# Scores from transposed projections: query and key layout taken from the token-wise product, squares on GpSimd

## What is computed

```
q = split_heads(tokens @ Wq, HEADS)
kv = split_heads(tokens @ Wkv, HEADS)
k, v = (kv[..., :DK], kv[..., DK:])
q, k, v = (l2norm(q), l2norm(k), l2norm(v))
sim = jnp.einsum('bhid,bhjd->bhij', q, k)
attn = jnp.square(jax.nn.relu(sim))
out = jnp.einsum('bhij,bhjd->bhid', attn, v)
out = tanh_norm(out)
return out @ Wout
```

## Time and profile before

| | |
|---|---|
| three runs | 568.56, 570.13, 570.86 us (median 570.13) |
| the profiled execution | 570.36 us, of which 568.4 us are the span from the first to the last instruction |
| attention | about 22 to 229 us of the span, after a head of 22 us |
| busy in the whole span | PE 93%, DVE 75%, ACT 66%, POOL 58% |
| busy from 97 to 122 us (25.0 us) | PE 23.9, DVE 20.5, ACT 18.5, POOL 14.9 us |
| one batch in the steady stretch | 26.88 us (score(13) starts at 98.76, score(17) at 125.64) |

### The profile page before, as it was taken

One profiled execution on the slowest core, in us unless ns is written; L12 is line 12 of the kernel. 1 busy time (PEld: TensorE's weight loads), 2 busy tenths in 40 slices (PEclk: granted clock), 3 DMA queues, 4 the chain that ended last, 5 costly groups with the idle time before them and its releaser, 6 DMA issues. The chain is left out here.

```text
span 568.4 us, 10116 instructions
## 1 busy us (share of the span) xinstructions
PE 529.2 (93%) x3280; PEld 399.7 (70%) x3280; DVE 428.1 (75%) x1004; ACT 376.8 (66%) x675; POOL 327.7 (58%) x277
## 2 busy tenths in 40 slices
PE   5798799999999998899999999999999999999996
PEld 4565467576666665586887877887887887888884
DVE  5966978888879687559679778778778778777664
ACT  5697868777778875264465864864864864755653
POOL 2643929384856564186565756656656655565553
PEclk9899989999999999799999999999999999999999
DMA  8200000000000002910192761851851851861920
GB/s 227 81 18 15 21 15 17 15 15 15 16 16 22 11 21 76 211 29 1 36 217 52 174 132 30 197 104 28 201 101 29 200 118 31 189 127 50 215 56 18
DMA packets 36083, 44.73 MB, mean 79 GB/s; under 512 B 5440, under 2 KB 18880, under 8 KB 36032
## 3 DMA queue, kind: packets, MB, share of 16 engines
q1 hardware_dynamic: 31616, 42.53, 32.9%
q10 hardware_dynamic: 4416, 1.57, 1.2%
HBM read 40.94 MB, written 3.15 MB: 78 GB/s over the span
## 5 line engine op out<-in xcount | busy, mean ns | idle before, releaser
L493 POOL TENSOR_TENSOR hl<-hb,hh 128x512 fp32r<-128x512 f32 x128 | 165.4, 1293 | 137.7 <-ACT hh L703 134.7
L696 ACT ACTIVATE sil<-PS 128x512 f32<-128x512 f32 (+1 forms) x136 | 80.9, 595 | 90.1 <-PE PS L1196 89.3
L1075 DVE TENSOR_TENSOR PS<-sil,PS 128x512 f32<-128x512 f32 x128 | 88.4, 690 | 62.4 <-PE PS L1196 41.4
L1196 PE MATMUL PS<-fxh,wfh 128*128 128x512 f32 x264 | 104.9, 397 | 1.7 <-issue 1.7
L1196 PE MATMUL PS<-fxl,wfh 128*128 128x512 f32 x264 | 104.6, 396 | 0.0
L1196 PE MATMUL PS<-fxh,wfl 128*128 128x512 f32 x264 | 104.3, 395 | 0.0
L703 ACT ACTIVATE hh<-hb 128x512 fp32r<-128x512 f32 x128 | 80.2, 627 | 28.2 <-DVE hb L1080 27.8
L1080 DVE TENSOR_TENSOR hb<-PS,wbc 128x512 f32<-128x512 f32 x128 | 88.5, 691 | 9.2 <-DMA wbc<-w_dram 2.5
L854 DVE SCALAR_TENSOR_TENSOR aT<-PS,rl 128x1024 f32<-128x1024 f32 x64 | 75.2, 1217 | 9.1 <-ACT rl L559 9.1
L559 ACT ACTIVATE rl<-PS 128x1024 f32<-128x1024 f32 x64 | 62.3, 1031 | 22.3 <-PE PS L1196 21.7
L418 POOL TENSOR_TENSOR sr<-n2o,half 128x32 f32<-128x32 f32 x7 | 38.2, 5463 | 51.1 <-DVE n2o L861 51.1
(11 more groups left out here) (168 smaller groups left out, 905.8 us busy)
## 6 DMA issues: line engine op xcount, KB each, us to landing
wbc<-w_dram SPq DMA_DIRECT2D x48, 512.0 KB, 11.7
wbc<-w_dram SPq DMA_DIRECT2D x32, 128.0 KB, 2.9
wbc<-w_dram SPq DMA_DIRECT2D x16, 256.0 KB, 4.3
wfs<-wf_dram SPq DMA_DIRECT2D x32, 98.0 KB, 1.9
band_dram<-zero SPq DMA_DIRECT2D x16, 80.0 KB, 1.7
band<-band_dram ACTq DMA_DIRECT2D x4, 320.0 KB, 3.0
out_dram<-X SPq DMA_DIRECT2D x4, 256.0 KB, 2.3
X<-x_dram SPq DMA_DIRECT2D x1, 896.0 KB, 7.7
```

Of the source, the lines that this page charges most:

```text
L493: g.tensor_tensor(hl[:, n % RING, :], hb[:, n % RING, :], hh[:, n % RING, :].bitcast(F32), ALU.subtract).then_inc(F("hl"), 1)
L696: s.activation(sil[0:rows, n % 2, :], PS[0:rows, G0 + n % 2, :], ACT.Silu).then_inc(F("silu"), 1)
L1075: v_.tensor_tensor(PS[:, bank, :], sil[:, n % 2, :], PS[:, bank, :], ALU.mult).then_inc(F("t"), 1)
L1196: return nc.tensor.matmul(o, w, m, start=start, stop=stop)
```

## The change

The second projection goes. ACT copies the token-wise product to a new SBUF tile `qkt` (`keep_pairs`): queries into 32-wide slots whose other halves POOL has set to zero once, keys side by side. PE transposes 128 × 128 pieces of `qkt` into PSUM: four transposes for each `group(n, j)` in place of six products. The squares are no longer made by ACT from PSUM: for batches 1 to 7 POOL makes them from `qkt` (`square_pairs`, four instructions of 256 columns per batch); for batch 0 ACT makes them as before, after its copies (`first_square_pairs`). `pair_norms` on DVE moves from behind `squares(4b + 1)` to behind `squares(4b + 2)`. 768 columns of weights are neither loaded nor split any more. The keys stand in another order, so `vc` is read through another view.

```diff
@@ POOL
+            g.memset(qkt[:, :, 0:NG * QG], 0.0).then_inc(cs("qkz"), 1)
             g.memset(Fpad[:, :, :], 0.0).then_inc(cs("fpad"), 1)
...
+            def square_pairs(n, t):
+                pool.wait_ge(A("qkc"), 2 * n + t + 1)
+                pool.wait_ge(A("n2q"), 2 * (n - 1) + t + 1)
+                g.tensor_tensor(by_head(sqqk[:, t, 0:QK]), q_heads(t), q_heads(t), ALU.mult).then_inc(A("sqq"), 1)
+                pool.wait_ge(*freed("qk", n, t))
+                g.tensor_tensor(sqqk[:, t, QK:2 * QK], k_heads(t), k_heads(t), ALU.mult).then_inc(A("sqq"), 1)
...
                 if b + 2 < B:
                     inverse_deviation(b + 2)
+                if b + 1 < B:
+                    square_pairs(b + 1, 0)
+                    square_pairs(b + 1, 1)
                 if b:
                     output_norms(b - 1)
@@ ACT
-            def square_pairs(n, t):
+            def keep_pairs(n, t):
                 act.wait_ge(*full("qk", n, t))
-                after(act, A("n2q"), 2 * (n - 1) + t + 1)
-                s.activation(sqqk[:, t, :], PS[:, bank_of("qk", n, t), :], ACT.Square).then_inc(free_of("qk", n, t), 1)
+                if n:
+                    act.wait_ge(*full("g", n - 1, NQ - 1))
+                    after(act, A("sqq"), 4 * (n - 2) + 2 * t + 2)
+                bank = bank_of("qk", n, t)
+                s.activation(q_heads(t), by_head(PS[:, bank, 0:QK]), ACT.Copy).then_inc(A("qkc"), 1)
+                signal = free_of("qk", n, t) if n else A("qkk0")
+                s.activation(k_heads(t), PS[:, bank, QK:2 * QK], ACT.Copy).then_inc(signal, 1)
+
+            def first_square_pairs(t):
+                s.activation(sqqk[:, t, :], PS[:, bank_of("qk", 0, t), :], ACT.Square).then_inc(free_of("qk", 0, t), 1)
...
-            first_weights_high(3)
...
-            square_pairs(0, 0)
-            square_pairs(0, 1)
+            act.wait_ge(cs("qkz"), 1)
+            for t in range(2):
+                keep_pairs(0, t)
+            for t in range(2):
+                first_square_pairs(t)
             square_values(0, 1)
@@ DVE
             def pair_norms(n, t):
-                dve.wait_ge(*freed("qk", n, t))
+                if n:
+                    dve.wait_ge(A("sqq"), 4 * (n - 1) + 2 * t + 2)
+                else:
+                    dve.wait_ge(*freed("qk", 0, t))
...
                 squares(NG * b + 1)
-                if more:
-                    pair_norms(n, 0)
-                    pair_norms(n, 1)
...
                 squares(NG * b + 2)
                 if more:
+                    pair_norms(n, 0)
+                    pair_norms(n, 1)
                     value_norms(n, 0)
                     clear_norms(n, 0)
@@ PE, group(n, j)
                 for part in range(2):
-                    cols = slice((2 * j + part) * P, (2 * j + part + 1) * P)
-                    last = split3(PS[:, bank, part * L:(part + 1) * L], wah[:, cols], wal[:, cols],
-                                  xTh[:, :], xTl[:, :])
+                    cols = k_cols(part) if j == 1 else q_cols(j + part)
+                    for t in range(2):
+                        last = nc.tensor.transpose(PS[:, bank, part * L + t * P:part * L + (t + 1) * P], qkt[:, t, cols],
+                                                   ident[:, :])
                 last.then_inc(done, 1)
```

More of the change, by code:

```diff
@@ L202, in hybrid_layer @@
         Z = Sems(ctx, nc, "full0 full5 full6 full7 free0 free5 free6 free7")
-        ld = Sems(ctx, nc, "in_x0 in_x in_wv0 in_wv1 in_wq in_wp in_wo in_wf0 in_wf1 in_sd in_gw in_wb in_bb zeroed")
-        cs = Sems(ctx, nc, "id0 id half rid ind0 ind rm rf sel fpad zero sel1 sdz wah wal wfh wfl sdh sdl")
-        A = Sems(ctx, nc, "stats mv ve rstd xn xTh vraw sqv n2v n2q nm nm_v rr vi vc0 vc vp S relu a av Oc sqO "
+        ld = Sems(ctx, nc, "in_x0 in_x in_wv0 in_wv1 in_wp in_wo in_wf0 in_wf1 in_sd in_gw in_wb in_bb zeroed")
+        cs = Sems(ctx, nc, "id0 id half rid ind0 ind rm rf sel fpad zero sel1 sdz wah wal wfh wfl sdh sdl qkz")
+        A = Sems(ctx, nc, "stats mv ve rstd xn xTh vraw sqv n2v n2q nm nm_v rr vi vc0 vc vp qkc qkk0 sqq S relu a av Oc sqO "
                           "sr sr_half n th nmx rec f1 ff fhi f")
@@ L299, in hybrid_layer, with q_cols, k_cols, q_heads @@
         fxh, fxl, wbc = (fxh0, fxh1), (fxl0, fxl1), (wbc0, wbc1)
+        def q_cols(g):
+            return slice(QG * g - DK * (g % 2), QG * g - DK * (g % 2) + P)
+        def k_cols(f):
+            return slice(NG * QG + f * P, NG * QG + (f + 1) * P)
+        def q_heads(t):
+            slots = qkt[:, t, 0:NG * QG].rearrange("p (g x) -> p g x", x=QG)[:, :, 0:P]
+            return slots.rearrange("p g (r y) -> p g r y", y=SLOT)[:, :, :, 0:DK]
+        def k_heads(t):
+            return qkt[:, t, NG * QG:QT]
+        def by_head(x):
+            return x.rearrange("p (g r d) -> p g r d", g=NG, r=HG)
+        def k_by_group(x):
+            return x.rearrange("p (f r a) -> p f a r", f=2, r=HG)
+        def heads_by_group(x):
+            return x.rearrange("p (f a r) -> p f a r", f=2, a=2)
         block = ctx.enter_context(nc.Block())
@@ L1231, in group @@
             def group(n, j):
+                for t in range(2):
+                    if j != 1:
+                        pe.wait_ge(A("qkc"), 2 * n + t + 1)
+                    elif n:
+                        pe.wait_ge(*freed("qk", n, t))
+                    else:
+                        pe.wait_ge(A("qkk0"), t + 1)
                 bank, done = turn("g", n, j)
                 for part in range(2):
[L1234 to L1236 removed]
+                    cols = k_cols(part) if j == 1 else q_cols(j + part)
+                    for t in range(2):
+                        last = nc.tensor.transpose(PS[:, bank, part * L + t * P:part * L + (t + 1) * P], qkt[:, t, cols],
+                                                   ident[:, :])
                 last.then_inc(done, 1)
@@ L1560, in layout @@
     wk, wv = wkv[:, :, :DK], wkv[:, :, DK:]
[L1561 to L1566, removed]
+    wa = np.concatenate([wq, wk.reshape(D, 2, 2, HG, DK).transpose(0, 1, 3, 2, 4).reshape(D, H * DK), wv.reshape(D, H * DV)], axis=1)
     eg = np.asarray(L0_ffn_expert_gate).transpose(2, 0, 1).reshape(D, E * I)
```

24 lines of the change are left out of this document (11 added, 13 removed).

## The result

The changed kernel takes **579.68 us** (median of four runs, 577.89 to 581.10); the kernel before, on the same chip, 570.41 (568.56 to 570.86). The ratio is 1.0167, with a 95% interval from 1.0129 to 1.0205: slower by 9.3 us. The forecast was 577.5 with a range from 572.0 to 583.5. The profiled execution took 580.3 us, of which 578.5 are span, 10.1 more than before.

What follows compares the result with a forecast made beforehand. The prediction took DVE's late add to X, not PE, as the bound. Head 1.85, batch 0 1.15, batch 1 0.55 and batches 2 to 6 3.6 sum to 7.15 us: 570.36 becomes 577.5, range 572.0 to 583.5.

Steps and rivals of the forecast that it cites:

- What bounds the kernel: Between 112 and 119 us of a batch a late DVE lengthens it; PE work saved ahead of 119 us gains nothing.
- the ring: DVE's first sqv sum, ACT's second squares, DVE's second sum: the moved sums' 1.18 us pass on, 1.15 at the add.
- Transposes at 0.48 us for a group: Four transposes replace 0.91 us of products; only group(n, 2) counts, saving 0.43, so batches 2 to 6 lose 0.72 each.
- Batch 0: PE waits for aT ahead of score(4), so all of the delay counts and no saving: +1.15 us.
- Batch 1: score(8) and relu(8) come 1.15 us late; 0.55 is left where PE waits for DVE: +0.55 us.
- The head: Before score(0): POOL's clearing delays DVE by 0.8 us, ACT's four copies add 1.03 at sqv; together +1.85.
- The signs named ahead: Profile after: second sqv sum 3.6 us behind aT, PE's wait near 2 us, steady batch 27.6, POOL idle near 3.
- POOL's squares free: Four instructions at 0.7 us end at 106.6, with 2.9 us in hand ahead of sr: cost nothing; slow-squares rival 0.06.
- What ends behind the add: output_factors' first small step (L866) starts later but ends at nearly the same time, with POOL's values: nothing more.
- the gap's case: Rival, chance 0.15: DVE's gap between its sqv sums takes up the moved sums; 573.4 us, 572.7 with a cheap clearing.
- The clock: Rival, chance 0.25: PE's 2.2 us idle in batches 2 to 6 drops the clock, 5 × 1.1 us more: 583.0.
- took the feed-forward for unchanged: The change leaves the feed-forward layers as they are; a changed time there would show the prediction wrong.

Runs made afterwards that it cites:

- e1: Kernel before with only pair_norms moved behind squares(4b + 2); products, ACT's squares and head as before: 577.08 us, ratio 1.0145.
- e9: Kernel before with a second buffer for the values' squares and nothing else: 569.71 us, ratio 1.0027.
- e4: Changed kernel with the transposes of groups 0 and 1 of each later batch issued three times over into the same bank: 575.95 us, ratio 1.0135.
- e10: Kernel before with a second buffer for the values' squares and ACT's second squares ahead of keep_output(4b + 1): 566.63 us, ratio 0.9969.
- e3: Changed kernel with POOL's clearing of qkt moved behind the first inverse deviation: 579.22 us, ratio 1.0196.
- e8: Changed kernel with each of POOL's four squares per batch made three times over: 580.23 us, ratio 1.0227.
- e7: Changed kernel with only POOL's clearing of qkt moved behind the third split of weights on DVE: 578.46 us, ratio 1.0186.
- e6: Changed kernel with pair_norms behind normalise, a second buffer for the values' squares, and POOL's clearing behind the third split of weights: 569.04 us, ratio 1.0004.
- e11: Changed kernel with pair_norms behind normalise, two value-square buffers, clearing behind the third weight split, ACT's second squares ahead of keep_output(4b + 1): 567.32 us, ratio 0.9980.
- e12: As e11, with DVE's weight_low(4b + 1) moved behind squares(4b + 3) and the add to X: 567.75 us, ratio 1.0010.

## Why the prediction was right, point by point

- **What bounds the kernel.** DVE between the first sum over `sqv` and the add to X, not PE. Held: with the sums back PE is idle for 0.94 us there, and 48 matmuls fewer did not make the kernel faster.
- **The delay goes through the ring whole.** Forecast 1.15 us at the add to X; in e1 PE's wait grew by 1.14, and the second buffer took out the gap. Held for the changed kernel. What the prediction read out of the kernel before, that DVE's own sum starts the squares it then waits for, is only half of it: there ACT's own list ends at the same time, since the second buffer alone gained nothing (e9).
- **Transposes at 0.48 us for a group.** Group(n, 2) to the score is 0.56 (128.22 to 128.78), and PE starts 0.42 us behind the start of the add to X where it started 0.33 behind. So the third group is worth 0.35 − 0.09 = 0.26 us a batch, not 0.43. This term was too large: batches 2, 4 and 6 are 0.87, 0.92 and 0.73 longer, and batches 3 and 5 without the clock 0.86 and 0.90. Together 4.28, forecast 3.6. The figure of the Trainium skill (TensorE: Matmul & The Clock Gate, Part 4: PE-mode transpose), 275 ns each, would have given 1.10 for a group; the trace does not bear it out.
- **Batch 0.** Forecast 1.15, measured 1.11. **Batch 1.** Forecast 0.55. Two runs without a fall of the clock in these batches price it: score(4) to score(8) is 25.37 us in e4 and 24.24 before; score(8) to score(10) 13.04 in e4 and 13.61 in e10 (that e10 stands there for the kernel before at full clock is an estimate: the two differ only in the gap on DVE). 1.13 − 0.57 = 0.56. Held.
- **The head.** Forecast 1.85 = 0.8 + 1.03. The first transposes come 0.85 later, and from the last product to score(0) it is 4.12 − 3.09 = 1.03 more. The other 0.11 of 1.99 go with the time at which PE's products change speed. The sizes held, but the way to the 0.8 was another: DVE was not seen to wait for `ind0`; its four `sel` steps took 1.67 us under the clearing (0.67 in e3, where only two clearings of 0.31 and 0.15 us ran beside them), and the next step follows without idle time. The clearing held them up as well as `ind`, which ends at 3.03. The trace does not part the two. Who moves only the order on POOL meets the same thing one step later, as e3 did.
- **The signs named ahead.** The second sum over `sqv` starts 3.5 us behind the end of `aT` (forecast 3.6; 118.84 + 1.22 = 120.06, and 123.57), PE waits 2.06 us ahead of group(n, 2) (near 2), the steady batch at full clock is 27.75 us (27.6), read from e4 and e8, since in the changed kernel's own profile batches 3 and 5 hold a fall.
- **POOL's squares free.** They start 0.57 us apart, forecast 0.7, and 3.45 us are left ahead of `sr`, forecast 2.9. Held, with room for eight more. They do lengthen DVE's normalising step beside them to 1.08 us (112.85) from 0.59, but DVE waits 3.10 us for PE behind it.
- **What ends behind the add.** The step that took 1.40 us in the earlier trace rows (L866, now L912) takes 0.28 and ends at 128.27. POOL's scaling of the values ends at 126.33 + 1.91 = 128.24, 0.03 us ahead of it as before (120.46 and 120.49). Nothing came from there, as forecast.

The terms without the clock give 1.88 + 1.11 + 0.56 + 4.28 = 7.8 us, forecast 7.15. One slip in the prediction changes nothing here: it takes 572.0 as the low end of the gap's case, which by its own sum is 572.7.

- **The clock, held as a rival at 0.25, was partly true.** It fell behind the add's wait in two of five batches: behind 2.06 us at 98.93 and 2.48 us at 156.39, not behind 2.06 at 128.22 and 185.74 or 0.99 at 213.68. In batch 1 it was at the lower level for longer than before. Against e4's 13.04 and e10's 13.61 the stretch from score(8) to score(10) lost 2.67 us in the changed kernel (15.71) and 1.13 in the kernel before (14.74). With 0.11 in the head, 0.17 between score(4) and score(8) (25.54 against e4's 25.37) and the two falls of 1.54 and 1.55 it is 0.11 + 0.17 + 1.54 + 1.54 + 1.55 = 4.9 us more than before, and then 2.6 less at the entry of the feed-forward: 2.3 net, which with 7.8 is the 10.1 of the spans. What the sum had wrong is that it put the clock at nothing and took the feed-forward for unchanged: its work did not change, its clock did. The rival's 5 × 1.1 was wrong in its count (two of five, not five), yet the 4.9 us lost in the attention are near its 5.5. That the time came out only 2.2 us above the forecast is in part luck: the 2.6 us won back belong to a fall that the profiled execution of the kernel before had and that of the changed one had not.
- **What stays open.** How often the clock falls at each place differs between executions: behind the same wait of 2.06 us at batch 2 it fell in the profile of e7 and not in that of e8. What share of the medians' 9.3 us the clock has, stays open within a few us. The kernel before alone shows how much the clock moves a time: of its 69 executions measured beside the experiments, the 16 with a mean granted clock of 0.997 took 565.9 to 567.8 us, the 24 with 0.988 or less 570.0 to 571.6. The four beside the changed kernel lay high (median 570.41). The changed kernel with a small move in its head (e3, e7) stands at 1.0196 and 1.0186 against medians of 568.7 and 568.6. So the whole loss is 9 to 11 us.

## What to carry to other kernels

An instruction moved ahead of a point where two engines hand one buffer to each other can cost its whole length, even where the trace shows idle time on its engine between the hand-overs, because that idle time is started by the engine itself. Here 1.14 of 1.18 us came through. Ask of each wait who starts the work that ends it, and how far behind the next condition stands: in e6, e11 and e12 a cause of a wait was removed, and no steady batch became more than 0.07 us shorter (26.63, 26.56 and 26.58 us), since the next cause stood right behind it. Idle time of TensorE behind such a wait is not neutral, since it can be followed by a stretch at the lower clock; with the transposes of two groups made three times over (e4) the profiled kernel was at full clock from 28 us to 572 us and no slower.

## What the runs showed of the hardware that was not expected

- POOL held DVE up. Two normalising steps of DVE took 0.60 us with POOL idle (5.74 in the changed kernel's head), 1.13 beside a clearing of 1.06 us on POOL, and 1.08 beside POOL's squares (112.85). Four `sel` steps took 0.67 us beside two short clearings (e3) and 1.67 beside the long one. A step on 32 columns took 1.40 and 0.28 us, ending both times 0.03 us behind POOL's scaling of the values, and 0.17 once that was over (156.17, beside one of POOL's powers). POOL's own steps did not become longer: the clearing took 1.06 us in each of its three places. The Trainium skill (SBUF — State Buffer, Who interferes with whom) says that a tensor_scalar step in its two-port mode and a GpSimd instruction shut one another out for a whole instruction. The trace agrees in kind: each of these stretches of DVE steps came out longer by 0.5 to 1.2 us, never by more than the POOL instructions beside it lasted. Whether the steps ran in that mode, no row shows.
- In the fourteen profiles of this case PE's products in the head went from 0.63 to 0.40 us at between 10.4 and 14.2 us, with the same products ahead, the first of which started between 7.1 and 8.1 us. One score(0) against another tells no more than about 1 us.
- Products of 512 columns took 0.63 us with the clock at its lower level (1.2 GHz; 232 to 233 us in the kernel before, granted 0.50) and 0.40 at the upper (2.4 GHz); the starts were 0.43 and 0.23 apart.
